# GNN edge phase with dense edge tiles at fixed addresses, and a segment sum over (tile, block) visits with a ring of message tiles

## The chip, the cores and the metric

The kernel runs on one core of a Trainium2 chip. The metric is the device time of one execution in microseconds (us). The kernel before took 1274.54 us (median of three runs, 1274.37 to 1276.86).

## The reference

Layer norm of x (1250 nodes x 512), one message-passing layer over 20,000 edges sorted by their destination node, then a small mixture-of-experts part. All is in float32. The part that matters here is the message layer:

```python
edge_feat = jnp.concatenate([x[src], x[dst], edge_attr], axis=-1)
h = mish(edge_feat @ W1 + b1)
messages = mish(h @ W2 + b2)
agg = jax.ops.segment_sum(messages, dst, num_segments=x.shape[0])
u = mish(jnp.concatenate([x, agg], axis=-1) @ W3 + b3)
```

## The kernel before

Four phases follow one another with a barrier of all engines between them: `prologue`, `edge_phase`, `node_phase` and `ffn_phase`. The change touches the first two.

**Tiles.** The nodes lie in 10 blocks of 125. The edges are worked on in tiles of 128. Before, each tile holds edges of one block only, so every block begins a new tile and its last tile may be partly empty: 20,000 edges need at most `TILES` = 166 tiles, that is 83 pairs (`PAIRS`), and the loops always run over all 83. The DVE works out in the prologue where each tile starts (`tiles_reached`, `tile_blocks`, `tile_starts`, L488 to L509): `start_i`, `block_i` and `block_off`.

**Prologue.** It normalises x and makes two tables in DRAM, `src_table` = x @ W1[src part] and `dst_table` = x @ W1[dst part] + b1 (PE L581 to L600, ten row tiles; ACT L404 and DVE L558 evict, SP L260 and L263 store). GpSimd copies the edge attributes and the indices to DRAM scratch (L336, L337), with a tail of padding (L299, L300).

**Edge phase.** It is one pipeline of steps s, written out in full for every engine, from `FIRST` = -5 to `LAST` = `PAIRS` + 4 = 87. Each step works at several pairs at different stages. For the pair p:
- SP at s = p - 5 reads the two tile starts into registers (L684) and issues for each tile one load of indices (L685) and two of edge attributes (L687).
- GpSimd gathers rows of `src_table` at s = p - 2 (L702) and adds rows of `dst_table` at s = p - 1 (L709). The gather buffer has three slots and a slot is free when PE has transposed it (`gath_read`).
- PE transposes the attributes at s = p - 1 (L897), transposes the gathered rows into the PSUM banks of linear 1 at s = p (`gathered_bank`, L836) and adds the attribute product (L870, L871). The second half of the banks waits for `summed`, since segment sums of an earlier pair are in that bank.
- ACT and DVE compute mish for linear 1 (DVE L813, L786, L806, L818) and for linear 2 (DVE L821, L809, L826).
- PE does linear 2 with split high and low parts at s = p + 1 (`hi_tile` of the second tile) and s = p + 2 (`hi_tile` of the first, both `lo_tile`; L841, L844).
- DVE rounds the message (`msg_hi`, L826), and DVE (L801) and GpSimd (L717) make the low parts `msg_lo`, two buffers of two tiles each.
- The segment sum is at s = p + 4: DVE makes a one-hot matrix from the local destination numbers (`dloc`, L790, and L795), PE multiplies it with the two parts of the message (L882, L883), and DVE adds the result to the block's rows of `agg`: `add_sums(m, 0)` in the same step, `add_sums(o, 1)` of the pair before early in the next step. Each `add_sums` first reads the block number from SBUF into a register (L769), then waits for the sum, then adds (L774).

At the end of the phase W3 is loaded (L690) and split into high and low parts: ACT L764, DVE L829, GpSimd L720, spread over the last steps by `act_parts`, `dve_parts` and `pool_parts`.

**Order of the work around the change.** PE in one step: `hi_tile(g, 0)`, first half of the gathered banks, second half (after `summed`), `lo_tile(g, 0)`, the eight attribute matmuls, `lo_tile(g, 1)`, the four sum matmuls, `hi_tile(r, 1)`, two attribute transposes. DVE in one step: L781, `add_sums(o, 1)`, L786, L790, L795, L801, L806, L809, L813, `add_sums(m, 0)`, L818, L821, L826. GpSimd in one step: two L702, two L709, one L717.

## Time and profile before

| | us |
|---|---|
| median of three runs | 1274.54 |
| lowest, highest | 1274.37, 1276.86 |
| the profiled execution, its time | 1276.67 |
| its span in the trace | 1275.1 |
| PE busy | 1120.8 (88%) |
| DVE busy | 990.7 (78%) |
| ACT busy | 874.9 (69%) |
| GpSimd busy | 739.4 (58%) |

All times are of one profiled execution, in us unless marked ns. PE is the TensorE matmul stream, PEld its weight loads (they overlap matmuls), DVE the VectorE, ACT the ScalarE, POOL the GpSimd, SPq, DVEq and PEldq the instruction queues of their engines. In the rows, L and a number is a line of the kernel. "[0.59 <-issue]" behind a row says how long the engine had stood idle before it and what ended that; "issue" means that nothing which the trace shows was waited for. Matmuls are pipelined: each row of a 512-column matmul shows about 0.39 us, but one starts 0.23 us after the other. The edge phase runs from 97.7 to 924 us of the span.

### The profile page before, as it was taken

To read this page: it belongs to the slowest core of one execution; us is meant where nothing else is said; L and a number is where in the kernel's file an instruction comes from. 1 tells how busy PE (TensorE), PEld (TensorE's weight loads), DVE (VectorE), ACT (ScalarE), POOL (GpSimd) and SP (SyncE) were. 2 spreads that over 40 slices of the span, in tenths; PEclk is the share of its full clock that TensorE was granted. 3 is DMA by queue.
4 is the path that set the end of the run, shared out by engine and by line. 5 is a ranking of instruction groups with operands and counts; after the bars stand their busy time and mean duration, and the time that the engine had idled before them with its cause. 6 is when DMAs were issued, how large, how long until landed. Compare 5 with 4: busy or idle time off the path is not lost. (4 is left out here: it accounts for less than half of the span.)

```text
span 1275.1 us, 21174 instructions
## 1 busy us (share of the span) xinstructions
PE 1120.8 (88%) x5823; PEld 911.8 (72%) x5824; DVE 990.7 (78%) x1793; ACT 874.9 (69%) x1061; POOL 739.4 (58%) x589
## 2 busy tenths in 40 slices
PE   3991999999999999999999999999579995679974
PEld 2761788888878888888888888888357774568863
DVE  6640699999999999999999999999848875643356
ACT  2211798999989999999899998999544541433332
POOL 3235677777777777777777777773221210644420
PEclk9995999999999999999999999999779995669975
DMA  5725666666666666666666666664020112734435
GB/s 164 271 89 124 141 128 125 130 124 129 128 126 129 125 128 127 126 131 124 128 127 128 130 127 125 129 123 116 0 67 25 49 38 68 212 88 132 132 121 182
DMA packets 138654, 153.51 MB, mean 120 GB/s; under 512 B 80635, under 2 KB 89226, under 8 KB 138477
## 3 DMA queue, kind: packets, MB, share of 16 engines
q0 software_dynamic: 40912, 101.69, 37.9%
q1 hardware_dynamic: 97629, 50.66, 15.5%
q8 instruction: 42, 0.69, 0.2%
q14 instruction: 55, 0.45, 0.1%
q10 hardware_dynamic: 16, 0.02, 0.0%
HBM read 141.74 MB, written 15.66 MB: 123 GB/s over the span
## 5 line engine op out<-in xcount | busy, mean ns | idle before, releaser
L702 POOL DMA_INDIRECT gath<-src_table,idx_sl x166 | 223.6, 1347 | 143.0 <-PE ps L836 84.9
L709 POOL DMA_INDIRECT gath<-dst_table,idx_sl x166 | 274.8, 1655 | 50.4 <-issue 50.4
L841 PE MATMUL ps<-W2h,hTh 128*128 128x512 f32 x664 | 262.6, 395 | 0.0
L841 PE MATMUL ps<-W2l,hTh 128*128 128x512 f32 x664 | 262.2, 395 | 0.0
L841 PE MATMUL ps<-W2h,hTl 128*128 128x512 f32 x664 | 188.5, 405 | 0.0
L717 POOL TENSOR_TENSOR msg_lo<-act,msg_hi 128x512 fp32r<-128x512 f32 x83 | 152.5, 1837 | 33.2 <-DVE msg_hi L826 33.2
L774 DVE TENSOR_TENSOR agg<-agg,ps 125x512 f32 x166 | 114.0, 687 | 57.8 <-issue 42.9
L841 PEld LDWEIGHTS ps<-W2l,hTh 128*128 128x128 f32 x664 | 124.7, 188 | 29.2
L841 PEld LDWEIGHTS ps<-W2h,hTh 128*128 128x128 f32 x664 | 125.1, 188 | 26.3
L733 ACT ACTIVATE act<-ps 128x1024 f32<-128x1024 f32 x83 | 85.2, 1027 | 72.0 <-issue 47.0
L836 PE MATMUL ps<-ident,gath 128*128 128x128 f32 x664 | 103.6, 282 | 29.2 <-DMA gath<-dst_table,idx_sl 14.6
L841 PEld LDWEIGHTS ps<-W2h,hTl 128*128 128x128 f32 x664 | 113.0, 189 | 15.5
L836 PEld LDWEIGHTS ps<-ident,gath 128*128 128x128 f32 x664 | 77.3, 142 | 58.7 <-DVE agg L774 26.3
L786 DVE SCALAR_TENSOR_TENSOR act<-act,ps 128x1024 f32<-128x1024 f32 x83 | 100.8, 1214 | 2.1 <-ACT act L752 2.1
L809 DVE SCALAR_TENSOR_TENSOR act<-act,ps 128x1024 f32<-128x1024 f32 x83 | 100.6, 1212 | 2.1 <-ACT act L761 2.0
L818 DVE TENSOR_TENSOR hTl<-act,hTh 128x1024 fp32r<-128x1024 f32 x83 | 101.0, 1217 | 0.0
L744 ACT ACTIVATE act<-act,half_col 128x1024 f32<-128x1024 f32 x83 | 95.8, 1154 | 2.7
L758 ACT ACTIVATE act<-act,half_col 128x1024 f32<-128x1024 f32 x83 | 95.6, 1152 | 2.7
L742 ACT ACTIVATE act<-act 128x1024 f32<-128x1024 f32 x83 | 88.1, 1062 | 3.8 <-issue 2.8
L761 ACT ACTIVATE act<-act 128x1024 f32<-128x1024 f32 x83 | 88.1, 1062 | 2.6
L755 ACT ACTIVATE act<-act 128x1024 f32<-128x1024 f32 x83 | 87.0, 1049 | 3.5 <-DVE act L821 3.5
L752 ACT ACTIVATE act<-act 128x1024 f32<-128x1024 f32 x83 | 87.4, 1053 | 0.0
(315 smaller groups left out, 2589.3 us busy)
## 6 DMA issues: line engine op xcount, KB each, us to landing
f_w_raw<-in_L_ffn_w_dram SPq DMA_DIRECT2D x32, 512.0 KB, 4.7
ea_sl<-ea_scr SPq DMA_DIRECT2D x332, 32.0 KB
ea_scr<-in_edge_attr_dram POOLq DMA_DIRECT2D x1, 5000.0 KB
w_raw<-in_L_gnn_W_dram SPq DMA_DIRECT2D x3, 1024.0 KB, 13.2
idx_sl<-idx_scr SPq DMA_DIRECT2D x166, 1.5 KB
gath<-src_table,idx_sl POOLq DMA_INDIRECT x166
gath<-dst_table,idx_sl POOLq DMA_INDIRECT x166
x_raw<-in_x_dram SPq DMA_DIRECT2D x5, 448.0 KB
```

Of the source, the lines that this page charges most:

```text
L702: pool.indirect_dma_start(out=gath[:, k, j, :], out_offset=None, in_=src_table[:, :], in_offset=bass.IndirectOffsetOnAxis(ap=idx_sl[:, p % ...
L709: pool.indirect_dma_start(out=gath[:, k, j, :], out_offset=None, in_=dst_table[:, :], in_offset=bass.IndirectOffsetOnAxis(ap=idx_sl[:, p % ...
L717: nc.gpsimd.tensor_tensor(msg_lo[:, p % 2, 1], act2[:, p % A2, 1], f32(msg_hi[:, p % 2, 1]), ALU.subtract).then_inc(S["msg_lo1_ready"], 1)
L742: nc.scalar.activation(a1, a1, ACT.Square).then_inc(S["sq1"], 1)
L744: nc.scalar.activation(a1, a1, ACT.Ln, bias=half_col[:], scale=0.5).then_inc(S["ln1"], 1)
L758: nc.scalar.activation(a2, a2, ACT.Ln, bias=half_col[:], scale=0.5).then_inc(S["ln2"], 1)
L774: nc.vector.tensor_tensor(row, row, sums(p)[0:NB, j, :], ALU.add).then_inc(S["summed"], 1)
L786: nc.vector.scalar_tensor_tensor(out=h, in0=h, scalar=1.0, in1=ps_1[:, r % 2], op0=ALU.subtract, op1=ALU.mult).then_inc(S["h_ready"], 1)
L809: nc.vector.scalar_tensor_tensor(out=a3, in0=a3, scalar=1.0, in1=ps_2[:, f % 2], op0=ALU.subtract, op1=ALU.mult).then_inc(S["msg_ready"], 1)
L818: nc.vector.tensor_tensor(hTl[:, r % 2], h, f32(hTh[:, r % 2]), ALU.subtract).then_inc(S["h_lo"], 1)
L836: ins = nc.tensor.matmul(ps_1[:, p % 2, d, j * P:(j + 1) * P], lhsT=gath[:, p % GA, j, d * P:(d + 1) * P], rhs=ident[:], is_transpose=True ...
L841: return nc.tensor.matmul(ps_2[:, p % 2, j, :], part[:, p % 2, d, j * P:(j + 1) * P], weights[:, d, :], start=False, stop=last)
```

## The change

- The edges are laid out densely: tile t is edges 128t to 128t + 127, without regard to blocks. `TILES` is now 158, so `PAIRS` is 79. The addresses of a tile's loads are known when the program is built; SP reads no register and issues one load of indices and two of attributes for a pair instead of two and four.
- A tile may hold edges of more than one block. The segment sum therefore runs over `VISITS` = 166 (tile, block) pairs, 83 pairs of visits (`SUMS`). All stages but the sum run over 79 pairs, the sums over 83, and `LAST` stays 87.
- A message tile can be needed by later visits, so `msg_hi` and `msg_lo` are rings of 14 tiles. The ring slot of each visit (`slot_i`) is read by PE into a register, two reads a step, ahead of the gathered banks; the sum matmuls address their moving operand with it.
- The local destination numbers `dloc` of all visits are made once, in the prologue: a DRAM copy of the destinations by tile (`dst_scr`), two indirect gathers of its rows by visit on GpSimd, two DVE copies, two PE transposes and one DVE subtraction. The DVE instruction L790 of every step goes away, and with it SP's wait on it.
- To make room for the rings, `eaT`, `ea_sl` and `act1` lie over the W3 high part and `hTh`, `hTl` over the W3 low part. The splitting of W3 waits for their last use, and its parts are ordered anew over the last steps.

```diff
@@ constants @@
-TILES = (EDGES + BLOCKS * (P - 1)) // P
+TILES = 2 * ((EDGES + 2 * P - 1) // (2 * P))
+ROWS = TILES * P
+VISITS = TILES + BLOCKS - 2
+VISITS += VISITS % 2
+RING = 14
@@ gnn_ffn_kernel @@
-        ea_scr = dram("ea_scr", (EDGES + P, EDIM), F32)
-        idx_scr = dram("idx_scr", (EDGES + P, 3), I32)
+        ea_scr = dram("ea_scr", (ROWS, EDIM), F32)
+        idx_scr = dram("idx_scr", (ROWS, 2), I32)
+        dst_scr = dram("dst_scr", (TILES, P), I32)
...
-        start_i = sb("start_i", [P, TILES], I32, edge_ctx)
-        block_i = sb("block_i", [P, TILES], I32, edge_ctx)
-        block_off = sb("block_off", [P, TILES], F32, edge_ctx)
+        slot_i = sb("slot_i", [P, VISITS], I32, edge_ctx)
+        block_i = sb("block_i", [P, VISITS], I32, edge_ctx)
+        dloc = sb("dloc", [P, VISITS], F32, edge_ctx)
@@ prologue: gpsimd @@
-                c.inc(nc.gpsimd.tensor_copy(rec_i[:, :, 2], dst_i[:]))
...
+                    pool.dma_start(dst_flat[0:EDGES].rearrange("(p j) -> p j", p=EP), dst_i[:]).then_inc(S["dst_out"], 16)
...
-            pool.wait_ge(S["tail_out"], 32)
+                pool.wait_ge(S["dst_out"], 16)
+            pool.wait_ge(S["tail_out"], 48)
...
+            pool.wait_ge(S["col_ready"], 1)
+            for n, rows in enumerate(VISIT_PARTS):
+                pool.indirect_dma_start(out=vdst_i[0:rows, n, :], out_offset=None, in_=dst_scr[:, :],
+                                        in_offset=bass.IndirectOffsetOnAxis(ap=tile_col[0:rows, n:n + 1], axis=0)).then_inc(S["vdst_in"], 16)
@@ prologue: vector @@
-            def tile_starts():
...
+            def visit_tiles():
+                c.step(nc.vector.tensor_reduce(out=behind[:], in_=reached[:].rearrange("p b v -> p v b"), axis=AX_X, op=ALU.add))
+                c.inc(nc.vector.tensor_tensor(tile_f[:], iota_v[:], behind[:], ALU.subtract))
+                c.inc(nc.vector.tensor_tensor(slot_f[:], iota_s[:, 0:VISITS], behind[:], ALU.subtract))
                 c.inc(nc.vector.tensor_copy(block_i[:], block_f[:]))
                 c.inc(nc.vector.tensor_scalar(block_off[:], block_f[:], float(NB), None, ALU.mult))
                 c.wait()
+                nc.vector.tensor_scalar(tile_f[:], tile_f[:], float(TILES - 1), None, ALU.min).then_inc(S["tiles_set"], 1)
+                c.step(nc.vector.tensor_scalar(wrap_f[:], slot_f[:], 0.0, float(RING), ALU.is_lt, ALU.mult))
+                c.step(nc.vector.tensor_tensor(slot_i[:], slot_f[:], wrap_f[:], ALU.add))
+            def visit_columns():
+                dve.wait_ge(S["col_ps"], 1)
+                for n, rows in enumerate(VISIT_PARTS):
+                    ins = nc.vector.tensor_copy(tile_col[0:rows, n:n + 1], ps_m[0:rows, 128 + n:129 + n])
+                ins.then_inc(S["col_ready"], 1)
+            def visit_nodes():
+                dve.wait_ge(S["vdst_in"], 32)
+                for n, rows in enumerate(VISIT_PARTS):
+                    ins = nc.vector.tensor_copy(vdst_f[0:rows, n, :], vdst_i[0:rows, n, :])
+                ins.then_inc(S["vdst_ready"], 1)
+                dve.wait_ge(S["vdst_ps"], 1)
+                c.step(nc.vector.tensor_tensor(dloc[:], ps_m[:, 256:256 + VISITS], block_off[:], ALU.subtract))
@@ prologue: tensor @@
-            steps(pe, step, 0, BLOCKS, 4, BLOCKS - 1)
+            steps(pe, step, 0, BLOCKS - 1, 4, BLOCKS - 3)
+            pe.wait_ge(S["tiles_set"], 1)
+            for n, rows in enumerate(VISIT_PARTS):
+                ins = nc.tensor.transpose(ps_m[0:rows, 128 + n:129 + n], tile_f[0:1, n * P:n * P + rows], ident[0:1, 0:1])
+            ins.then_inc(S["col_ps"], 1)
+            step(0, BLOCKS)
+            pe.wait_ge(S["vdst_ready"], 1)
+            for n, rows in enumerate(VISIT_PARTS):
+                ins = nc.tensor.transpose(ps_m[:, 256 + n * P:256 + n * P + rows], vdst_f[0:rows, n, :], ident[0:rows, 0:rows])
+            ins.then_inc(S["vdst_ps"], 1)
@@ edge_phase @@
+        def over_w3h(name, shape, part):
+            return nc.alloc_sbuf_tensor_at(name, shape, F32, offset=T["w3h_at"] + part * HID * 4)
+        idx_sl = sb("idx_sl", [P, IN, 2, 2], I32)
+        eaT = w3h[:, 0, :].rearrange("p (s e) -> p s e", s=2)
+        ea_sl = over_w3h("ea_sl", [P, IN, 2, 2 * EDIM], 1)
         gath = sb("gath", [P, GA, 2, HID])
-        act1 = sb("act1", [P, 2, KC, E2])
         act2 = sb("act2", [P, A2, 2, HID])
-        hTh = sb("hTh", [P, 2, KC, E2], F32R)
-        hTl = sb("hTl", [P, 2, KC, E2], F32R)
-        msg_hi = sb("msg_hi", [P, 2, 2, HID], F32R)
-        msg_lo = sb("msg_lo", [P, 2, 2, HID], F32R)
-        dloc = sb("dloc", [P, TILES])
+        msg_hi = sb("msg_hi", [P, RING, HID], F32R)
+        msg_lo = sb("msg_lo", [P, RING, HID], F32R)
...
+        hTh, hTl = half_of(w3l, 0), half_of(w3l, KC)
+        act1 = over_w3h("act1", [P, 2, KC, E2], KC)
...
-        FIRST, LAST = -5, PAIRS + 4
+        SUMS = VISITS // 2
+        FIRST, LAST = -5, SUMS + 4
...
+        def visited(m):
+            return 0 <= m < SUMS
+        def ring(p):
+            return slice(2 * p % RING, 2 * p % RING + 2)
+        def ring_free(p):
+            return p - 1 if 2 * p >= RING else 0
...
-        act_parts = {PAIRS: (7, 0, 1, 2), PAIRS + 1: (3, 4, 5, 6)}
-        dve_parts = {PAIRS + 1: (0, 1), PAIRS + 2: (2,), PAIRS + 3: (3, 4, 5, 6)}
-        pool_parts = {PAIRS + 1: (7,)}
+        act_parts = {PAIRS: (0, 1, 2, 3), PAIRS + 1: (4, 5, 6, 7)}
+        dve_parts = {PAIRS + 2: (0, 1), PAIRS + 3: (2, 3), PAIRS + 4: (4, 5)}
+        pool_parts = {PAIRS + 3: (7, 6)}
@@ edge_phase: sync, gpsimd @@
-                        sp.wait_ge(S["dst_ready"], p - IN + 1)
-                    for j in range(2):
-                        first = sp.value_load(start_i[0:1, p * 2 + j:p * 2 + j + 1], min_val=0, max_val=EDGES)
-                        sp.dma_start(idx_sl[:, k, j, :], idx_scr[bass.ds(first, P), :]).then_inc(idx_in[k], 16)
-                        for half in range(2):
-                            sp.dma_start(ea_sl[:, k, j, half * EDIM:(half + 1) * EDIM], ea_scr[bass.ds(first, P), :]).then_inc(ea_in[k], 16)
+                    edges = slice(p * E2, (p + 1) * E2)
+                    sp.dma_start(idx_sl[:, k], idx_scr[edges, :].rearrange("(j p) r -> p j r", p=P)).then_inc(idx_in[k], 16)
+                    for half in range(2):
+                        sp.dma_start(ea_sl[:, k, :, half * EDIM:(half + 1) * EDIM], ea_scr[edges, :].rearrange("(j p) d -> p j d", p=P)).then_inc(ea_in[k], 16)
...
-                    pool.wait_ge(*loaded(idx_in, IN, p, 32))
+                    pool.wait_ge(*loaded(idx_in, IN, p, 16))
...
-                    if p >= 2:
-                        pool.wait_ge(S["sum_ps"], p - 1)
-                    nc.gpsimd.tensor_tensor(msg_lo[:, p % 2, 1], act2[:, p % A2, 1], f32(msg_hi[:, p % 2, 1]), ALU.subtract).then_inc(S["msg_lo1_ready"], 1)
+                    need(pool, S["sum_ps"], ring_free(p))
+                    nc.gpsimd.tensor_tensor(msg_lo[:, ring(p)][:, 1], act2[:, p % A2, 1], f32(msg_hi[:, ring(p)][:, 1]), ALU.subtract).then_inc(S["msg_lo1_ready"], 1)
                 for w in pool_parts.get(s, ()):
+                    pool.wait_ge(S["lin2_ps"], PAIRS)
@@ edge_phase: vector @@
-                if exists(l):
-                    dve.wait_ge(*loaded(idx_in, IN, l, 32))
-                    nc.vector.tensor_tensor(dloc[:, 2 * l:2 * l + 2], idx_sl[:, l % IN, :, 2], block_off[:, 2 * l:2 * l + 2], ALU.subtract).then_inc(S["dst_ready"], 1)
-                if exists(m):
-                    dve.wait_ge(S["dst_ready"], m + 1)
+                if visited(m):
...
                     dve.wait_ge(S["msg_hi_ready"], m + 1)
-                    if m >= 2:
-                        dve.wait_ge(S["sum_ps"], m - 1)
-                    nc.vector.tensor_tensor(msg_lo[:, m % 2, 0], a4[:, 0], f32(msg_hi[:, m % 2, 0]), ALU.subtract).then_inc(S["msg_lo0_ready"], 1)
+                    need(dve, S["sum_ps"], ring_free(m))
...
-                if exists(m):
+                if visited(m):
...
-                    if f >= 2:
-                        dve.wait_ge(S["sum_ps"], f - 1)
+                    need(dve, S["sum_ps"], ring_free(f))
                     dve.wait_ge(S["msg_ready"], f + 1)
-                    nc.vector.tensor_copy(msg_hi[:, f % 2], a3).then_inc(S["msg_hi_ready"], 1)
+                    nc.vector.tensor_copy(msg_hi[:, ring(f)], a3).then_inc(S["msg_hi_ready"], 1)
                 for w in dve_parts.get(s, ()):
+                    dve.wait_ge(S["lin2_ps"], PAIRS)
@@ edge_phase: tensor @@
                 if exists(g):
                     hi_tile(g, 0)
+                if visited(m):
+                    slots = [pe.value_load(slot_i[0:1, 2 * m + j:2 * m + j + 1], min_val=0, max_val=RING - 1) for j in range(2)]
...
                     lo_tile(g, 1).then_inc(S["lin2_ps"], 1)
-                if exists(m):
+                if visited(m):
                     pe.wait_ge(S["onehot_ready"], m + 1)
-                    pe.wait_ge(S["msg_lo0_ready"], m + 1)
-                    pe.wait_ge(S["msg_lo1_ready"], m + 1)
+                    pe.wait_ge(S["msg_lo0_ready"], min(m + 1, PAIRS))
+                    pe.wait_ge(S["msg_lo1_ready"], min(m + 1, PAIRS))
                     pe.wait_ge(S["h_ready"], min(m + 4, PAIRS))
                     o = sums(m)
                     for j in range(2):
-                        nc.tensor.matmul(o[0:NE, j, :], onehot[:, m % 2, j, :], msg_hi[:, m % 2, j, :], start=True, stop=False)
-                        ins = nc.tensor.matmul(o[0:NE, j, :], onehot[:, m % 2, j, :], msg_lo[:, m % 2, j, :], start=False, stop=True)
+                        for lo, part in enumerate((msg_hi, msg_lo)):
+                            ins = nc.tensor.matmul(o[0:NE, j, :], onehot[:, m % 2, j, :], part[:, bass.ds(slots[j], 1), :].rearrange("p a n -> p (a n)"),
+                                                   start=lo == 0, stop=lo == 1)
                     ins.then_inc(S["sum_ps"], 1)
```

## Rows read from the trace of the kernel before

**Rows 1.** Busy time by stretch: window, length, PE, PEld, DVE, ACT, POOL, PE clock, DMA share, GB/s

```profile
200.00:872.20 672.20, 662.05 (x3442) 540.97 (x3441) 619.20 (x931) 614.69 (x646) 529.22 (x359) 1.00 0.65 127
...
915.00:920.00 5.00, 1.90 (x4) 1.17 (x4) 3.00 (x5) 0.00 (x0) 1.64 (x1) 0.50 0.00 0
```

**Rows 2.** Timeline of DVE: start, length, engine, line, operation; the first sum's addition of three steps

```profile
159.36 0.69 DVE L774 TENSOR_TENSOR agg<-agg,ps 125x512 f32 x1 [0.23 <-PE ps L883]
...
872.23 0.69 DVE L774 TENSOR_TENSOR agg<-agg,ps 125x512 f32 x1
...
881.26 0.69 DVE L774 TENSOR_TENSOR agg<-agg,ps 125x512 f32 x1 [0.23 <-PE ps L883]
```

**Rows 3.** Timeline of all engines over one step of the edge phase

```profile
506.24 0.69 DVE L774 TENSOR_TENSOR agg<-agg,ps 125x512 f32 x1
...
508.40 1.68 POOL L709 DMA_INDIRECT gath<-dst_table,idx_sl  x1 [0.30 <-issue]
...
509.30 0.43 DVE L781 TENSOR_TENSOR eaT<-ps,eaT 64x256 fp32r<-64x256 f32 x1
...
510.31 0.69 DVE L774 TENSOR_TENSOR agg<-agg,ps 125x512 f32 x1 [0.59 <-issue]
510.34 1.37 PE L836 MATMUL ps<-ident,gath 128*128 128x128 f32 x8
...
511.06 0.42 PEld L836 LDWEIGHTS ps<-ident,gath 128*128 128x128 f32 x4 [0.35 <-DVE agg L774]
```

**Rows 4.** Line L769, DVE's register reads in two stretches: ns min/median/max, first and last start

```profile
L769 DVEq TENSOR_LOAD <-block_i x1: 943/943/943, 508.9 to 508.9; - x1
...
L769 DVEq TENSOR_LOAD <-block_i x1: 300/300/300, 874.9 to 874.9; - x1
```

**Rows 5.** PE's register reads of the last phase (L1691), all and one, and the matmuls around

```profile
L1691 PEldq FUSED_REGOPS  x56: 42/151/168, 1130.4 to 1221.0; - x56
L1691 PEldq TENSOR_LOAD <-expert_i x35: 297/303/493, 1129.8 to 1220.7; - x35
...
L1691 PEldq TENSOR_LOAD <-expert_i x1: 310/310/310, 1151.8 to 1151.8; - x1
...
1152.20 0.28 PE L1718 MATMUL f_ps_n<-w1Th,xgTl 128*128 x1
1152.72 0.52 PE L1698 MATMUL f_ps_t<-ident,xg 128*128 128x128 f32 x3 [0.24 <-issue]
```

**Rows 6.** Timeline of the start of the edge phase

```profile
98.72 0.40 SPq L685 DMA_DIRECT2D idx_sl<-idx_scr  x1
...
101.53 0.34 SPq L685 DMA_DIRECT2D idx_sl<-idx_scr  x1
...
103.43 1.06 POOL L702 DMA_INDIRECT gath<-src_table,idx_sl  x1 [24.62 <-DMA idx_sl<-idx_scr]
...
111.47 1.61 POOL L709 DMA_INDIRECT gath<-dst_table,idx_sl  x1 [0.31 <-issue]
...
119.57 1.97 PE L836 MATMUL ps<-ident,gath 128*128 128x128 f32 x8 [14.61 <-DMA gath<-dst_table,idx_sl]
```

**Rows 7.** Timeline of DVE over the last steps of the edge phase

```profile
907.93 2.36 DVE L829 TENSOR_TENSOR w1l_w3l<-w_raw,w1h_w3h 128x512 fp32r<-128x512 f32 x2
...
917.32 0.68 DVE L801 TENSOR_TENSOR msg_lo<-act,msg_hi 128x512 fp32r<-128x512 f32 x1
920.29 0.69 DVE L774 TENSOR_TENSOR agg<-agg,ps 125x512 f32 x1 [2.29 <-PE ps L883]
920.90 2.49 DVE L829 TENSOR_TENSOR w1l_w3l<-w_raw,w1h_w3h 128x512 fp32r<-128x512 f32 x4
923.31 0.68 DVE L774 TENSOR_TENSOR agg<-agg,ps 125x512 f32 x1
```

**Rows 8.** Timeline of the end of the prologue

```profile
93.50 0.69 DVE L558 COPY tabs<-ps_b 125x512 f32<-125x512 f32 x1 [5.49 <-PE ps_b L600]
94.22 0.76 SPq L263 DMA_DIRECT2D dst_table<-tabs  x2
```

More of the change, by code:

```diff
@@ L481, in first_edges @@
[L481 removed]
+                c.step(nc.vector.tensor_copy(tfirst[:], cnt_i[:]))
+                c.step(nc.vector.scalar_tensor_tensor(out=shared[:], in0=tfirst[:], scalar=float(P), in1=first[:, 0:BLOCKS],
+                                                      op0=ALU.mult, op1=ALU.is_lt))
+                c.step(nc.vector.tensor_tensor_scan(out=extra[:], data0=ones[:, 0:BLOCKS], data1=shared[:], initial=0.0,
@@ L482, in first_edges @@
                                                     op0=ALU.mult, op1=ALU.add))
-                c.step(nc.vector.scalar_tensor_tensor(out=off[:], in0=tbase[:], scalar=-float(P), in1=first[:, 0:BLOCKS + 1],
-                                                      op0=ALU.mult, op1=ALU.add))
-                c.inc(nc.vector.tensor_tensor(doff[:], off[:, 1:BLOCKS + 1], off[:, 0:BLOCKS], ALU.subtract))
-            def tiles_reached():
-                for b in range(BLOCKS):
-                    c.inc(nc.vector.tensor_scalar(reached[:, b, :], iota_t[:], tbase[:, b + 1:b + 2], None, ALU.is_ge))
+                c.step(nc.vector.tensor_tensor(vbase[:], tfirst[:], extra[:], ALU.add))
```

105 lines of the change are left out of this document (62 added, 43 removed).

## The prediction

> **What bounds the kernel now.** I read the busy times by stretch first. Between 200 and 872.2 us PE is busy for 662 of 672 us at a granted clock of 1.00, DVE for 619 [rows 1]. So the edge loop is the place, and two engines are near full in it. The timeline of DVE gives its period: `add_sums(m, 0)` of step 4 starts at 159.36 and that of step 80 at 872.23 [rows 2], 76 steps apart, so a step takes 712.87 / 76 = 9.38 us. One step in the timeline shows what closes the loop [rows 3]. PE has its last sum matmul done, DVE adds the first sum at 506.24, works through L818, L821, L826 and L781 and adds the second sum only at 510.31. PE has begun the first half of the gathered banks at 510.34 and holds the second half until 511.06, released by that addition. From there it runs without a gap to the next sum. So the period is one PE half plus one DVE half. DVE stood 0.59 us idle before the second addition with nothing to wait for: its register read took 943 ns, from 508.9 on, where the same read takes 300 ns at 874.9 [rows 4], and the step from 872.23 to 881.26 is 9.03 us [rows 2]. Each pair of tiles costs one step, whatever it holds.
>
> **Part 1: four pairs fewer.** Loads, gathers, both linears and both mish run over 79 pairs instead of 83; the sums keep 83. `LAST` stays 87, so four steps of the full kind become steps with a sum alone. Four full steps go: 4 x 9.38 = 37.5 us [rows 2]. What replaces them is part 3.
>
> **Part 2: what is added to and taken from each remaining step.** L790 leaves DVE. It lay between the second addition and the first, where DVE has a wait on PE (0.23 us at two of the rows) [rows 2], so it is off the loop and I count 0. SP's register reads and half its DMAs go; SP's loads run pairs ahead: 0. The ring only moves waits on `sum_ps` that were long met: 0.
>
> PE gets two register reads a step, between `hi_tile(g, 0)` and the gathered banks. No row shows PE reading a register in this phase. The last phase does: the read takes 303 ns, the register operations after it 151 [rows 5], so a pair of reads is 2 x 0.45 = 0.91 us. They are in PE's instruction queue and not in the array. The question is whether that queue is far enough ahead. It is held by the wait on `summed` in front of the attribute transposes, met when the first addition ends, 506.24 + 0.69 = 506.93 [rows 3]. Then it issues 22 instructions (two transposes and nine matmuls with their weight loads). Four weight loads with their four transposes took 0.42 us, 0.052 each [rows 3], so it reaches the reads at 506.93 + 1.15 = 508.1 and is through at 509.0. The banks need it near 510.1, and before that it waits anyway for L781, which ends at 509.73 [rows 3]. Cover: 1.1 us. If both reads were as slow as DVE's worst (943 ns), they would end at 508.1 + 2 x (0.94 + 0.15) = 510.3; the first half of the banks would start 0.2 us late and the second half, held until 511.06, would not move. In the last phase a read began at 1151.8 while matmuls before it still started at 1152.20, so a read doesn't wait for the array; but the 0.24 us gap ahead of 1152.72 shows what it costs where the queue is only 0.4 us ahead [rows 5]. I take 0, with 0 to 0.1 us a step as the bounds of the forecast. A price far above is a rival below.
>
> The Trainium skill (TensorE: Matmul & The Clock Gate, the table at its head) gives TensorE a queue of 64 instructions; the 22 fit, and by it the sum stays as it is.
>
> **Part 3: the drain.** Steps 79 to 82 of the new kernel are like 83 to 86 of the old. The two L829 of step 84 (2.36 us [rows 7]) leave the path to step 86; one more comes in at step 85 (0.6), and I take 2.2 us as gained there, since the sum of step 85 waited for PE behind them: the addition at 920.29 would be at 918.1 in the old count. Then come four steps with a sum alone. In each, DVE's second addition of the pair before starts about 0.75 after the first (it waits for its end, 0.69), the one-hot matrix starts 0.60 after that and takes 0.41 (the distances of one step of DVE), and from the end of DVE's last input to the addition after the sum passed 920.29 - (917.32 + 0.68) = 2.29 us, with PE at half clock [rows 7, 1]. Sum: 0.75 + 0.60 + 0.41 + 2.29 = 4.05. PE's register reads are under that. In two of the steps two L829 lie in the chain too; alone four took 2.49, and beside GpSimd two took 2.36 [rows 7], so 1.2 to 2.4, taken as 1.8. The last first-addition is at 918.1 + 4 x 4.05 + 2 x 1.8 = 937.9, the phase ends at 937.9 + 0.75 + 0.68 = 939.3, where it ended at 923.31 + 0.68 = 924.0 [rows 7]. The drain costs 15.3 us. If PE held full clock, its four matmuls would start 0.23 apart instead of twice that and a step would be 0.9 shorter, with fast L829s 10.5 us in all; with slow ones and half a microsecond of exposed reads a step 18.5 us.
>
> **Part 4: the fill.** Before, GpSimd's first gather waits for the second index load, issued at 101.53, 2.8 us after the first at 98.72, and the register read ahead of the first took about 1 us. GpSimd starts 1.9 after that issue (103.43) [rows 6]. With one index load for a pair and no read, the gather starts at about 97.7 + 1.9 = 99.6, 3.8 us sooner. The second pair's indices no longer hold it back either, so the queue would reach L709 at 104.9, not 111.47. That one waits for its source gathers, about 4.6 us behind the end of their issue (as from the end of the second L709, 114.94, to PE at 119.57 [rows 6]): 102.0 + 4.6 = 106.6. All behind moves by 111.5 - 106.6 = 4.9 us. Bounds: 2.8 (the one issue alone) to 6.6.
>
> **Part 5: the prologue.** DVE has about 1 us of new small work in the tile tables and two copies, and had 5.49 us idle before its last eviction at 93.50 [rows 8]. So the two indirect gathers go out near 89, in 2.6 us of issue, and land near 94 to 95, by the 4.6 us above. Two DVE copies, two transposes and a subtraction follow, some 1.5 us: 96 to 96.5. The barrier is held by SP's last table store, issued at 94.22 and over near 97.5, since the first index load stands at 98.72 behind a read [rows 8, 6]. Covered; PE's two tiny transposes ahead of its last row tile shift that store by 0.3 to 0.5. I take +0.5; if the gathers land 3 us later the chain ends the phase: up to +3.5.
>
> **Sum.** -37.5 + 0 + 15.3 - 4.9 + 0.5 = -26.6 us. The profiled execution took 1276.67, so 1250.1 for it; it is 2.1 us above the median of the runs, and against 1274.54 I predict 1247.9. With the bounds (drain 10.5 to 18.5, fill -6.6 to -2.8, prologue 0 to 3.5, PE reads 0 to 0.1 x 79 = 8) the forecast's own range is 1241 to 1264.
>
> **Rivals.**
> *PE's register reads stand in the way (slower).* If a read is served only when the matmuls ahead are done, the two start at the end of `hi_tile`, 510.34, and the banks at 511.25. The first half takes 0.25, the second starts at 511.5 instead of about 511.1: 0.45 us a step, 79 x 0.45 = 36 us, total 1248 + 36 = 1284. It turns the sign from 0.34 us a step on. For it: the gap at 1152.72. Against: the read at 1151.8 ran beside matmuls [rows 5]. Chance 0.12.
> The Trainium skill (DMA: Bandwidth & Descriptors, Latency and other measured facts) puts the floor of a tensor load at about 600 ns, twice the 303 ns in this trace. By it two reads take 1.5 us; the sum stays, since 508.1 + 1.5 is still ahead of 510.1, and this rival would cost 0.6 us a step more.
> *PE's reads lengthen DVE's (about the same).* They run at 508.1 to 509.0, DVE's at 508.9, and that one is on the loop. Half of its 0.64 us stretch again would be 0.32 x 79 = 25 us: 1273. No row speaks for it but the fact that DVE's read varies at all [rows 4]. Chance 0.05.
> *DVE's slow read goes away (faster still).* It is slow where GpSimd's second L709 runs (508.40 to 510.08 [rows 3]) and fast at 874.9, when no gather is issued. If the new timing parts the two, a step takes 9.03: 75 x 0.35 = 26 us, 1222. But GpSimd is paced by PE's banks in the same loop as before, so they should meet again. Chance 0.08.
> *It doesn't do what it says.* The counts 79 and 83 are constants of the program, so the steps must go; only the price of the rest can be wrong. No chance of its own.
>
> **How the numbers follow.** Forecast 0.75, rivals 0.12, 0.05 and 0.08. The range 1224 to 1269 holds the forecast, its slips beyond its own range, and part of the second and the third rival; left out are the slower rival and most of the fastest. About 0.2% (2.5 us) is what a measurement can tell from no change. Faster by more: 0.75 + 0.08 + 0.02 = 0.85; within: 0.03; slower: 0.12.
>
> **What the profile would show.** The first addition of step 4 to that of step 76 in 72 x 9.38 = 675 us; PE's second bank half still released by DVE's second addition, and the queue's reads over before L781 ends; sum-only steps 4 to 6 us apart at the end; L702 first at about 2 us behind the barrier; the barrier released by SP's store. The prediction falls if the step is over 9.7 us, or if the last steps take over 6 us each.

## The result, and the profile after

The changed kernel takes 1254.32 us (median of 4 runs, 1252.38 to 1255.62) where the kernel before takes 1274.5: a ratio of 0.9836, with a 95% interval of 0.9818 to 0.9854. The forecast was 1247.9, faster, with a range of 1224 to 1269. The profiled execution took 1255.11 us, its span is 1253.5 (before: 1275.1).

The edge phase first. Busy time by stretch in the changed kernel (window, length, PE, PEld, DVE, ACT, POOL, PE clock, DMA share, GB/s), to be laid beside [rows 1]:

```profile
200.00:833.70 633.70, 615.31 (x3211) 505.25 (x3211) 574.15 (x803) 571.63 (x603) 492.96 (x335) 1.00 0.63 125
890.00:902.00 12.00, 6.20 (x12) 3.47 (x12) 4.59 (x9) 0.00 (x0) 0.00 (x0) 0.50 0.00 0
```

PE is busy for 97.1% of the full steps, where it was for 98.5%, and DVE for 90.6% against 92.1%: both are a little emptier. The clock is 1.00 as before, so each step has become longer by idle time of the engines. The timeline of DVE (start, length, engine, line, operation) says by how much; these are the first sum's additions of steps 4, 76 and 77, as in [rows 2]:

```profile
151.41 0.69 DVE L845 TENSOR_TENSOR agg<-agg,ps 125x512 f32 x1 [0.20 <-PE ps L951]
...
833.79 0.69 DVE L845 TENSOR_TENSOR agg<-agg,ps 125x512 f32 x1 [0.20 <-PE ps L951]
842.76 0.69 DVE L845 TENSOR_TENSOR agg<-agg,ps 125x512 f32 x1 [0.21 <-PE ps L951]
```

(833.79 - 151.41) / 72 = 9.477 us a step, against 9.38. One such step in the timeline of all engines, for [rows 3]:

```profile
483.25 0.69 DVE L845 TENSOR_TENSOR agg<-agg,ps 125x512 f32 x1 [0.19 <-PE ps L951]
...
485.35 1.75 POOL L778 DMA_INDIRECT gath<-dst_table,idx_sl  x1 [0.30 <-issue]
485.48 0.36 SPq L754 DMA_DIRECT2D idx_sl<-idx_scr  x1
485.88 1.87 SPq L756 DMA_DIRECT2D ea_sl<-ea_scr  x2
486.31 0.43 DVE L852 TENSOR_TENSOR w1h_w3h<-ps,w1h_w3h 64x256 fp32r<-64x256 f32 x1
487.32 0.60 PE L902 MATMUL ps<-ident,gath 128*128 128x128 f32 x4
487.40 0.69 DVE L845 TENSOR_TENSOR agg<-agg,ps 125x512 f32 x1 [0.66 <-issue]
488.14 0.66 PE L902 MATMUL ps<-ident,gath 128*128 128x128 f32 x4 [0.22 <-DVE agg L845]
```

The loop is closed as it was (its period is one half of PE's step plus one half of DVE's): the second half of PE's gathered banks is released by DVE's second addition. That one comes 4.15 us after the first (4.07 before), with 0.66 us of idle time ahead of it in place of 0.59. And SP now issues the loads of a later pair at 485.48 and 485.88, alongside DVE's block read. Here are the register reads, DVE's in this step and at 850.9 to 852.0 (for [rows 4]), then both of PE's, which are new (name, count: ns min/median/max, first and last start):

```profile
L840 DVEq TENSOR_LOAD <-block_i x1: 1030/1030/1030, 485.9 to 485.9; - x1
...
L840 DVEq TENSOR_LOAD <-block_i x2: 303/306/309, 850.9 to 852.0; - x2
...
L925 PEldq TENSOR_LOAD <-slot_i x2: 297/304/310, 484.1 to 484.9; - x2
L925 PEldq FUSED_REGOPS  x2: 151/151/151, 484.5 to 485.3; - x2
```

PE's reads cost what [rows 5] said and are over at 485.5, before DVE's begins. DVE's has grown from 943 ns to 1030.

The start of the phase, for [rows 6, 8]:

```profile
93.14 0.76 SPq L283 DMA_DIRECT2D dst_table<-tabs  x2
...
96.75 0.39 SPq L754 DMA_DIRECT2D idx_sl<-idx_scr  x1
...
98.81 0.98 POOL L771 DMA_INDIRECT gath<-src_table,idx_sl  x1 [9.14 <-DMA idx_sl<-idx_scr]
...
104.51 1.60 POOL L778 DMA_INDIRECT gath<-dst_table,idx_sl  x1 [0.94 <-DMA gath<-src_table,idx_sl]
...
111.83 1.97 PE L902 MATMUL ps<-ident,gath 128*128 128x128 f32 x8 [11.31 <-DMA gath<-dst_table,idx_sl]
```

PE has its first gathered rows 7.74 us earlier than before, and the first addition of step 4 comes 159.36 - 151.41 = 7.95 us earlier. About one microsecond of that is the prologue's, whose last store is issued at 93.14, not 94.22. The start isn't the same in every execution: in eight traces of the changed kernel and its variants with all gathers and additions in place, step 4's first addition lies between 150.21 and 152.03. At the end stand the steps with a sum alone, in a form that the kernel before did not have:

```profile
893.53 0.69 DVE L845 TENSOR_TENSOR agg<-agg,ps 125x512 f32 x1 [2.36 <-PE ps L951]
894.43 0.69 DVE L845 TENSOR_TENSOR agg<-agg,ps 125x512 f32 x1 [0.21 <-DVE agg L845]
895.04 0.41 DVE L862 TENSOR_TENSOR onehot<-iota_n,dloc 128x252 fp32r<-128x252 f32 x1
895.60 0.79 PE L951 MATMUL ps<-msg_hi,onehot 128*126 x1 [2.21 <-DVE onehot L862]
...
897.81 0.69 DVE L845 TENSOR_TENSOR agg<-agg,ps 125x512 f32 x1 [2.36 <-PE ps L951]
```

The last two take 4.28 us each. PE idles 2.21 us of one until the one-hot matrix is there, and DVE idles 2.36 until PE has its four matmuls done at half clock. The phase ends at 902.99 + 0.69 = 903.68.

The account of the spans, in us:

| stretch | before | after | difference | forecast |
| --- | --- | --- | --- | --- |
| start to step 4's first addition | 159.36 | 151.41 | -7.95 | -4.9 + 0.5 |
| step 4 to step 80 (before), 76 (after) | 712.87 | 682.38 | -30.49 | -37.5 |
| from there to the end of the phase | 51.76 | 69.89 | +18.13 | +15.3 |
| the rest of the kernel | 351.11 | 349.82 | -1.29 | 0 |
| sum | 1275.1 | 1253.5 | -21.6 | -26.6 |

The 7 us missing in the second line are 0.098 us in each of 72 steps. That is what most of the experiments are about. The last line of the table explains 5.0 of the 6.4 us between forecast and median; most of the other 1.4 comes from the profiled execution before, which lay 2.1 us above its median, where the one after lay 0.8 above. All ratios below are to the kernel before, measured beside each run (medians of 1272.9 to 1274.5 us), and all "steps" are (first addition of step 76 - that of step 4) / 72 unless said otherwise.

### The profile page after: what moved, and what is told of

It reads as the page before. It is cut to its first block and busy times, and to the rows that moved or that the text cites. A ratio compares the mean times of both kernels' runs of the same rounds, so it can differ in the third digit from the quotient of the medians.

```text
span 1253.5 us, 19768 instructions
## 1 busy us (share of the span) xinstructions
PE 1084.6 (87%) x5651; PEld 884.2 (71%) x5652; DVE 958.0 (76%) x1678; ACT 837.7 (67%) x1025; POOL 713.5 (57%) x574
## 3 DMA queue, kind: packets, MB, share of 16 engines
q0 software_dynamic: 39280, 97.61, 36.2%
## 5 line engine op out<-in xcount | busy, mean ns | idle before, releaser
L907 PE MATMUL ps<-W2h,w1l_w3l 128*128 128x512 f32 x1264 | 426.6, 398 | 0.0
L778 POOL DMA_INDIRECT gath<-dst_table,idx_sl x158 | 265.2, 1679 | 48.6 <-issue 47.1
L771 POOL DMA_INDIRECT gath<-src_table,idx_sl x158 | 207.9, 1316 | 126.1 <-PE ps L902 86.0
L907 PEld LDWEIGHTS ps<-W2h,w1l_w3l 128*128 128x128 f32 x1264 | 227.3, 189 | 38.6
L907 PE MATMUL ps<-W2l,w1l_w3l 128*128 128x512 f32 x632 | 248.2, 393 | 0.0
L907 PEld LDWEIGHTS ps<-W2l,w1l_w3l 128*128 128x128 f32 x632 | 119.0, 188 | 27.2
L802 ACT ACTIVATE act<-ps 128x1024 f32<-128x1024 f32 x79 | 81.2, 1027 | 74.8 <-PE ps L939 74.8
L884 DVE TENSOR_TENSOR w1l_w3l<-act,w1l_w3l 128x1024 fp32r<-128x1024 f32 x79 | 96.2, 1218 | 0.0
L951 PE MATMUL ps<-msg_hi,onehot 128*126 x166 | 69.0, 416 | 22.9 <-DVE msg_lo L867 12.2
L830 ACT ACTIVATE act<-act 128x1024 f32<-128x1024 f32 x79 | 83.9, 1062 | 2.5
L811 ACT ACTIVATE act<-act 128x1024 f32<-128x1024 f32 x79 | 83.1, 1052 | 3.7 <-DVE act L879 3.6
L824 ACT ACTIVATE act<-act 128x1024 f32<-128x1024 f32 x79 | 83.0, 1051 | 3.5 <-DVE act L887 3.5
L821 ACT ACTIVATE act<-act 128x1024 f32<-128x1024 f32 x79 | 83.3, 1055 | 0.0
L808 ACT ACTIVATE act<-ps 128x1024 f32<-128x1024 f32 x79 | 81.2, 1028 | 0.0
```

The lines of the kernel that those rows point to most:

```text
L771: pool.indirect_dma_start(out=gath[:, k, j, :], out_offset=None, in_=src_table[:, :], in_offset=bass.IndirectOffsetOnAxis(ap=idx_sl[:, p % ...
L778: pool.indirect_dma_start(out=gath[:, k, j, :], out_offset=None, in_=dst_table[:, :], in_offset=bass.IndirectOffsetOnAxis(ap=idx_sl[:, p % ...
L830: nc.scalar.activation(a2, a2, ACT.Exp, scale=-1.0).then_inc(S["quot2"], 1)
L884: nc.vector.tensor_tensor(hTl[:, r % 2], h, f32(hTh[:, r % 2]), ALU.subtract).then_inc(S["h_lo"], 1)
L907: return nc.tensor.matmul(ps_2[:, p % 2, j, :], part[:, p % 2, d, j * P:(j + 1) * P], weights[:, d, :], start=False, stop=last)
```

## Experiments: what lengthens the step

**PE's register reads removed.**

```diff
-slots = [pe.value_load(slot_i[0:1, 2 * m + j:...], ...) for j in range(2)]
+slots = [(2 * min(m, PAIRS - 1) + j) % RING for j in range(2)]
```

> The changed kernel, with one thing taken out: TensorE reads no ring positions; its two reads of a step are replaced by constants (so the sums of tiles that lie in two blocks take the wrong message tile; the amount of work is the same). Full steps of the changed kernel are 9.48 us apart where 9.38 was predicted. Theory A (SyncE's DMA issues now lie on VectorE's second block read, and the reads of TensorE cost nothing): the step stays at 9.45 to 9.50 us and the execution at about 1255. Rival B (TensorE's two reads, 0.3 us each, lengthen VectorE's read or the path): the step goes back to 9.38, 72 x 0.10 = 7 us off, about 1248. If the reads were in the sum-only steps' chain too, those would be shorter than 4.28 us.

Measured: 1253.93 us, ratio 0.9849 (0.9832 to 0.9865), step 9.464. The sum-only steps went from 4.28 to 4.20. The reads take 0.01 us of a step and 0.08 of a sum-only one, so rival B fell.

**SP's issues held back, first try and second.** In both, SP gets one wait more ahead of its loads of pair p:

```diff
 sp.wait_ge(S["eaT_ps"], p - IN + 1)
+if p >= 10:                                        # second try: p >= 9
+    sp.wait_ge(S["summed"], 2 * (p - 10) + 2)      # second try: p - 9
```

> The changed kernel, with one wait more: SyncE issues the loads of a later pair only after VectorE's second addition of the step (in the changed kernel it issues them beside VectorE's second block read, which takes 1.03 to 1.10 us there against 0.94 to 0.97 before). Theory A (SyncE's issues lengthen that read): the read goes back to 0.94 to 0.97 us, the step to 9.38, the time by 7 us to about 1248. Rival B (it isn't SyncE): the read stays at 1.03 to 1.10 and the step at 9.48; about 1255. If the loads came too late for their pair, steps would show waits on them; they run pairs ahead, so I expect none.

Measured: 1253.99 us, ratio 0.9844 (0.9827 to 0.986), step 9.473. The wait asked for an addition of the step before and was always met, so SP's issues stayed where they were. The trial says nothing on its theory. The second one does:

> The changed kernel, with one wait more, a pair later than in the trial before, in which SyncE's issues had not moved (they still began 0.01 us after VectorE's second block read): SyncE now issues the loads of a later pair behind VectorE's second addition. Theory A (SyncE's issue, when it begins with the read, adds 0.1 us to it): the read goes from 1.07 back to 0.95 us, as in the three steps at 286.5, 817.7 and 827.0 of the changed kernel that took 0.93 to 0.96 (two of them without an issue of SyncE near); the step goes from 9.47 to 9.38, about 7 us off, 1247. Rival B: the read stays at 1.03 to 1.08 and the step at 9.47; 1254.

Measured: 1246.99 us, ratio 0.9798 (0.9777 to 0.9819). The additions of steps 4 and 76 stand at 151.76 and 826.03, a step of 9.365. The timeline shows SP behind the second addition; below it, DVE's reads between 200 and 800 us have a largest value of 967 ns, where the changed kernel has 1098:

```profile
483.45 0.69 DVE L847 TENSOR_TENSOR agg<-agg,ps 125x512 f32 x1 [0.57 <-issue]
...
484.23 0.36 SPq L756 DMA_DIRECT2D idx_sl<-idx_scr  x1
```

```profile
L842 DVEq TENSOR_LOAD <-block_i x128: 300/322/967, 201.0 to 797.1; - x128
```

and in the changed kernel:

```profile
L840 DVEq TENSOR_LOAD <-block_i x127: 299/317/1098, 201.4 to 798.7; - x127
```

Theory A stands: SP's issue beside the read was the 7 us. The slow reads are again at 0.95 us in the median, where the changed kernel has 1.07 and the kernel before 0.94, and (9.477 - 9.365) x 72 = 8.1 us are gone from the steps. By the times alone the gain is less sure: 7.3 us between the medians, 4.8 by the two ratios (0.9836 and 0.9798), whose intervals just meet. Before the change, SP stood there in register reads (L684, 508.5 to 509.1 in the step of [rows 3]) and issued its index load at 509.65, 0.7 us into DVE's read; the change removed those, and in nearly every step its issues moved to 0.4 us before the read's start and to the start itself.

**One gather of destination rows in a pair instead of two.** The range in L778 is cut to j = 0, and the waits on `both_gath` count 16 instead of 32.

> The changed kernel, with the second tile of each pair left without its gather of destination rows (its result is wrong for those edges; all other work is the same). It is the gather whose issue on GpSimd (1.7 us) lies on VectorE's second block read. Theory A (that issue is what makes the read slow, 0.3 us without it): the read falls to about 0.3 to 0.4 us and the step to 9.0 to 9.1, the time to about 1255 - 72 x 0.4 = 1226. Rival B (the read is slow for another reason, the table in memory or the operation before it): read about 1.0, step 9.48, about 1255. Rival C: the gather left is now issued later and lies on the read in its place: a read between 0.6 and 1.0.

Measured: 1253.39 us, ratio 0.9839 (0.9822 to 0.9855), step 9.468. My theory A fell: the read is as slow without GpSimd's issue beside it. Nor did C come true: the gather left was issued at 784.1 for 1.58 us, and the read began at 786.5. The lines of the gather and of the read say so, and the DMA share in two windows (columns as in the first fence) shows what did meet the read:

```profile
L778 POOL DMA_INDIRECT gath<-dst_table,idx_sl x1: 1576/1576/1576, 784.1 to 784.1; - x1
...
L840 DVEq TENSOR_LOAD <-block_i x1: 1084/1084/1084, 786.5 to 786.5; - x1
```

```profile
786.00:786.40 0.40, 0.40 (x4) 0.30 (x3) 0.40 (x2) 0.33 (x3) 0.00 (x0) 1.00 0.00 0
786.50:787.50 1.00, 1.00 (x6) 0.81 (x5) 0.86 (x2) 1.00 (x2) 0.49 (x1) 1.00 0.94 164
```

The DMA engines are idle until 786.4, and at 0.94 during the read: the rows of the gather begin to move 2.3 us after the start of its issue, just there.

**No gather of destination rows.**

```diff
-for j in range(2):
-    pool.indirect_dma_start(out=gath[:, k, j, :], in_=dst_table[:, :], ..., compute_op=ALU.add)...
```

> The changed kernel, with both gathers of destination rows left out (the rows gathered are those of the sources alone, so the result is wrong; TensorE, VectorE and ScalarE do the same work). In the trial with one gather left per pair, no issue of GpSimd lay near VectorE's second read (the last had ended 0.8 us before it), and yet it took 1.07 us. What was there each time is the data of the destination rows (packets of 2048 bytes, added to what is in memory), which begins to flow 0.1 us before the read. Theory A (the start of that flow holds the read): without it the second read takes 0.3 us, though SyncE still issues with it, and the step falls to 8.97 to 9.05, the time to about 1220. Rival B (SyncE's issue, or the data of the source rows, holds it): the read stays near 1 us and the step at 9.4 or more. Rival C: GpSimd, free earlier, issues the source rows' gathers onto the read, and the read is slow by these: between 0.3 and 1.

Measured: 1211.11 us, ratio 0.9514 (0.9495 to 0.9533), step 8.988. All reads are fast, though SP issues its index load at 406.17 and its attributes at 406.57, beside a read at 406.6:

```profile
L832 DVEq TENSOR_LOAD <-block_i x134: 299/304/317, 199.9 to 798.5; - x134
```

So SP's issue alone holds nothing. It adds 0.1 us to a read that is already held.

**Destination rows not added.** `compute_op=ALU.add` is taken out of L778.

> The changed kernel, in which the gathers of destination rows no longer add to the rows in memory but take their place (the sources' share of each edge is lost, so the result is wrong); number, order, addresses and size of all gathers are the same. The first block read of a step begins as the data of the source rows begins to flow (packets of 4096 bytes) and takes 0.31 us; the second begins as that of the destination rows does (2048 bytes, added) and takes 1.07. Theory A (the addition in memory is what holds the read): plain destination rows hold it no more than source rows do; the second read takes 0.3 us, the step is 8.97 to 9.05, the time about 1220. Rival B (any flow that starts beside that read holds it, or GpSimd's issue or SyncE's does, and the first read is only lucky in its place): the read stays at 0.9 to 1.1 and the step at 9.38 to 9.48; about 1254.

Measured: 1218.7 us, ratio 0.9576 (0.956 to 0.9592), step 8.994.

```profile
L839 DVEq TENSOR_LOAD <-block_i x133: 299/307/326, 203.5 to 797.0; - x133
```

```profile
485.20:485.50 0.30, 0.30 (x3) 0.25 (x2) 0.30 (x2) 0.30 (x3) 0.30 (x1) 1.00 0.75 287
485.50:485.90 0.40, 0.40 (x4) 0.31 (x3) 0.40 (x1) 0.40 (x2) 0.09 (x1) 1.00 0.19 72
```

The sizes are as A expected, but the trial doesn't separate as cleanly as I meant: plain gathers are issued faster (1.02 us for the first, 1.57 before), so their rows had been moving for some time when the read came at 485.57. So no run puts a plain flow onto the second read itself. Other reads of the traces help. In the changed kernel, the first read of the next step does begin with a flow, that of source rows, which are not added, and takes 311 ns; the first reads of the other steps between 200 and 800 us take 0.30 to 0.32 as well. And in the kernel before there are reads that come when added rows have been moving for a while: that at 162.0, 0.7 us behind the first of them, takes 309 ns, and that at 621.8, 0.44 us behind the first, 556 ns.

The changed kernel, windows and read:

```profile
491.00:491.50 0.50, 0.50 (x4) 0.41 (x3) 0.50 (x1) 0.50 (x1) 0.20 (x2) 1.00 0.04 9
491.80:492.10 0.30, 0.30 (x3) 0.25 (x2) 0.30 (x2) 0.30 (x1) 0.30 (x1) 1.00 0.89 164
```

```profile
L840 DVEq TENSOR_LOAD <-block_i x1: 311/311/311, 491.8 to 491.8; - x1
```

The kernel before, windows and read:

```profile
161.00:161.30 0.30, 0.30 (x5) 0.21 (x3) 0.30 (x2) 0.30 (x1) 0.30 (x1) 1.00 0.15 20
161.70:162.00 0.30, 0.30 (x3) 0.25 (x2) 0.30 (x2) 0.30 (x2) 0.30 (x1) 1.00 0.83 143
```

```profile
L769 DVEq TENSOR_LOAD <-block_i x1: 309/309/309, 162.0 to 162.0; - x1
```

```profile
621.00:621.35 0.35, 0.35 (x5) 0.31 (x4) 0.35 (x1) 0.35 (x1) 0.35 (x1) 1.00 0.00 0
621.40:622.40 1.00, 1.00 (x6) 0.81 (x5) 0.97 (x3) 1.00 (x3) 1.00 (x1) 1.00 0.94 104
```

```profile
L769 DVEq TENSOR_LOAD <-block_i x1: 556/556/556, 621.8 to 621.8; - x1
```

Taken together: a block read that begins within 0.1 us of the first row of an added flow takes 0.88 to 1.1 us, and one that begins 0.45 us into it 0.56 to 0.71. One that begins 0.7 us into it takes 0.31 or 0.39 us, and one that meets no such beginning 0.3. All that are held end at about the same place: 1.0 to 1.05 us behind the flow's first row in the kernel before and in the trial above with SP's issues behind the addition, and 1.1 to 1.2 with SP's issues beside them. So it looks less like a read made longer by a fixed amount than like one held until the flow is about 1 us old. How the two are tied inside the chip no run here shows.

## Experiments: what a step and a read are worth

**DVE's block reads removed.** `b` becomes `(p * 2 + j) // 17`.

> The changed kernel, with VectorE's block reads taken out: the addition of a sum goes to block tile // 17, a constant (so some tiles are added to the wrong block; the work is the same). TensorE's reads stay. Theory A (the loop is one half of TensorE's step plus one half of VectorE's, and the latter contains the slow second read, about 1.05 us with what is behind it, at a VectorE that stands idle 0.7 us): the step falls to 9.38 - 0.35 = 9.0 us or a little under, as in the steps without gathers (8.97 to 9.03), and the time by 72 x 0.45 = 32 us or a little more, to about 1220. Rival: TensorE's own work (9.2 of 9.38 us busy) is the bound as soon as the read is gone, and the step falls only to 9.2 to 9.3: about 1240.

Measured: 1218.51 us, ratio 0.9569 (0.9553 to 0.9585), step 8.989. The slow read closes the loop, and behind it PE's own work is the bound at 8.99, below the 9.2 of the rival: PE has no gap left (columns as in the first fence).

```profile
200.00:790.00 590.00, 589.58 (x3154) 497.86 (x3153) 578.27 (x789) 561.53 (x592) 458.72 (x329) 1.00 0.66 132
```

**The kernel before with 158 tiles.** `TILES = 158`.

> The kernel before, with 158 tiles instead of 166 and nothing else changed (the edges of the last 8 tiles are left out). It measures the change's first part by itself, four full steps fewer: by the prediction's sum 4 x 9.38 = 37.5 us less, about 1237. With it the other terms of the change are the difference to 1254: the drain (+18), the step's +0.1 x 72, the fill (-8). If it comes out at 1250 or more, a step isn't the price of a pair and the sum is wrong at its base.

Measured: 1238.66 us where the kernel before took 1272.9 beside it, ratio 0.9729 (0.9711 to 0.9748): 34.2 us for four pairs. Its step is (837.85 - 159.46) / 72 = 9.422, 0.04 longer than the 9.38 before: its slow reads take 0.98 us in the median (up to 1.02), where they took 0.94. 4 x 9.38 = 37.5, less 72 x 0.042 = 3.0, is 34.5. Nothing in that program moved but the number of tiles; why its reads are 0.04 longer is open. The last 51.7 us are as before.

**The kernel before, with both reads of a pair early.**

```diff
+if exists(m):
+    read_blocks(m)          # both value_load of block_i, kept for add_sums
 if exists(p):
     dve.wait_ge(S["exp1"], p + 1)
```

> The kernel before, with both block reads of a pair moved: VectorE takes them together ahead of the first addition, in front of its wait for the first activation, and keeps the second value for the second addition. Nothing stands then between the attribute rows' low part and the second addition. Theory A (VectorE's slow second read closes the loop): the step falls from 9.38 to about 9.0, 76 x 0.37 = 28 us off, about 1246. Rival B: the early reads fall on another flow of gathered rows and are slow there too, and VectorE, with little slack, is late for the next wait of TensorE: a gain of 0 to 10 us. Rival C: TensorE is the bound at once: step 9.2, 1260.

Measured: 1246.72 us, ratio 0.9797 (0.9776 to 0.9818), step 9.026; between 200 and 800 us DVE's reads take 316 ns at most. This alone gives a little more than the change did (ratio 0.9797 against 0.9836, with intervals that meet at 0.9818). One early read, in one of the last steps with gathers, is slow:

```profile
L772 DVEq TENSOR_LOAD <-block_i x1: 650/650/650, 841.4 to 841.4; - x1
```

GpSimd had begun to issue a gather of destination rows at 839.40, and its first rows begin at 841.64, inside this read. So the new place is no protection by itself; it is good because the flows begin elsewhere.

**The changed kernel, with both reads early.** The same edit, under `visited(m)`.

> The changed kernel, with both block reads of a pair moved ahead of the first addition, in front of VectorE's wait for the first activation, as was done with the kernel before (there the step went from 9.38 to 9.03 us, the time from 1272.9 to 1246.7). Theory A (the data of the destination rows begins to flow at the place where the second read stood; at the new place no such flow begins): all reads take 0.3 us, SyncE's issues touch none of them, and the step is 8.99 to 9.03, as without any block read (8.99). That is 72 x 0.46 = 33 us under the changed kernel's 1254: 1219 to 1223. Rival B (the early reads of the changed kernel, whose GpSimd queue has another order of loads, meet the flow anyway): step above 9.2, over 1235.

Measured: 1222.37 us, ratio 0.9594 (0.9581 to 0.9608). The additions of steps 4 and 76 are at 151.58 and 800.48, a step of 9.012. Theory A again; the longest of the 166 reads takes 0.34 us.

**The changed kernel, one-hot matrices early in the drain.**

```diff
-if visited(m):
-    if m >= 2: dve.wait_ge(S["sum_ps"], m - 1)
-    ... onehot[:, m % 2] ...
+for v in ((m,) if m < PAIRS else ()) + ((m + 1,) if m + 1 >= PAIRS else ()):
+    if visited(v):
+        if v >= 2: dve.wait_ge(S["sum_ps"], v - 1)
+        ... onehot[:, v % 2] ...
```

> The changed kernel, with the one-hot matrix of the next pair made ahead of the first addition of this one in the steps that hold a sum alone (two buffers are there). In them the chain of the changed kernel is: second addition, one-hot matrix, four matmuls at half clock, first addition, 4.28 us a step, with TensorE idle for 2.2 us of each. Theory A (that chain sets the end of the phase): TensorE has its next matrix when it ends a sum, and a step takes about 2.1 to 2.6 us; four of them save 6 to 8 us, less what the two steps with the last weight parts keep (5.18 each, in which VectorE has 1.3 us more): about 1248. Rival B (TensorE's register reads or the weight parts bound these steps): no step under 3.5, a gain of under 3 us.

Measured: 1246.95 us, ratio 0.9788 (0.9774 to 0.9801); from step 76 to the end of the phase it is 61.05 us instead of 69.89. PE goes from sum to sum:

```profile
889.41 0.68 DVE L845 TENSOR_TENSOR agg<-agg,ps 125x512 f32 x1
889.64 0.79 PE L952 MATMUL ps<-msg_hi,onehot 128*126 x1 [0.67 <-DVE onehot L863]
...
891.65 0.79 PE L952 MATMUL ps<-msg_hi,onehot 128*126 x1
891.85 0.69 DVE L845 TENSOR_TENSOR agg<-agg,ps 125x512 f32 x1 [0.53 <-PE ps L952]
...
893.67 0.69 DVE L845 TENSOR_TENSOR agg<-agg,ps 125x512 f32 x1 [0.23 <-PE ps L952]
```

The last two steps take 2.44 and 1.82 us, those with weight parts 2.74 where I had them keep 5.18.

**Both edits in the changed kernel.**

> Both edits of the two kernels beside it in one: the block reads early, and the one-hot matrices early in the steps with a sum alone. They lie in different parts of the phase (the full steps, and the last steps), so their gains should add: about 33 + 6 = 39 us under the changed kernel, 1213 to 1217. Rival: the two share VectorE's wait in the last steps (the early reads stand ahead of the additions there too) and a part of the second gain is lost: 1218 to 1221.

Measured: 1214.12 us (1212.21 to 1215.07), ratio 0.9526 (0.9513 to 0.9539). It is 40.2 us under the changed kernel; the two edits alone gave 32.0 and 7.4 (by the ratios, which take out how the kernel before varied from run to run, 39.5, 30.8 and 6.1). So the gains add. It leaves nothing out, and is the fastest of all versions here that don't: 4.7% under the kernel before and 3.2% under the changed one.

## Why the prediction was right in sign and 6 us low

The result lies inside the forecast's own range of 1241 to 1264. By its steps:

- **Part 1, right in mechanism, 3 us too large in size.** Forecast -37.5, measured alone -34.2. The steps went as reckoned; the step that remained was not quite 9.38.
- **Part 2, PE's reads at 0: right.** The queue's cover was even larger than the 1.1 us of the sum: the reads of the step at 483.25 end at 485.5, and the banks' first weight load starts at 487.09. Taking the reads out moved the step by 0.01. (The 943 ns taken as DVE's worst read was not the worst: the kernel before has reads of up to 970.) The two rivals that hung on them, 1284 and 1273, have no part in the result. The first would have been 0.45 a step.
- **Part 2, SP at 0: this step failed.** I wrote that half of SP's DMAs go and that its "loads run pairs ahead: 0". That asked only whether a load comes too late, and not what its issue would lie beside once SP's reads ahead of it were gone. It came to lie on the one read of DVE that closes the loop. Measured: 0.1 us a step, 7 us, which SP's wait gave back (a step of 9.365, so what else the change does to a step, L790 and the ring among it, comes to about nothing, as forecast; 1246.99, under a microsecond from the forecast, though the errors of other terms offset each other in it: the start came out 3 us lower and the drain 2.8 higher than forecast).
- **The slow read named, its cause not.** The rival "DVE's slow read goes away" put it down to GpSimd's second gather issue, since it runs beside it in [rows 3]. It doesn't hang on that issue: with the issue away from it the read stayed slow, with the rows gone it was fast. Its size was right. I had 26 us and 0.35 a step for a fast read; the early reads gave 0.35 in the kernel before and 0.465 in the changed one.
- **Part 3, within its range, but 2.8 us short, and not where it was thought.** Sum-only steps were put at 4.05 and took 4.28: the second addition starts 0.90 after the first, not 0.75 (its read and wait add 0.21 idle), and PE's part took 2.36 from the end of the one-hot, not 2.29. They held half clock, as taken. The two with weight parts were put at 5.85 and took 5.18, so the four together were 0.9 us under the forecast. What was too small lies ahead of them: from step 76 to 82 the forecast had 918.1 - 872.23 = 45.9 us, and it took 883.17 - 833.79 = 49.4. I had counted 2.2 us as gained there by moving weight parts. The stretch up to 874.12 did gain 1.4 (7.31 us where 8.68 stood, 905.43 to 914.11), but the next one, up to 883.17, took 9.05 where its counterpart before (914.11 to 920.29) took 6.18. Two weight parts of DVE (L895, 2.35 us) stand in it ahead of the second addition, where one stood before (0.68), and the low part of the message (L867) takes 1.75 us beside GpSimd's weight parts (L789, 877.09 to 880.20), where it took 0.68. The total of 18.1 lies within 10.5 to 18.5.

```profile
874.12 0.69 DVE L845 TENSOR_TENSOR agg<-agg,ps 125x512 f32 x1 [0.64 <-PE ps L951]
...
875.33 2.35 DVE L895 TENSOR_TENSOR w1l_w3l<-w_raw,w1h_w3h 128x512 fp32r<-128x512 f32 x2
...
879.01 1.75 DVE L867 TENSOR_TENSOR msg_lo<-act,msg_hi 128x512 fp32r<-128x512 f32 x1
883.17 0.69 DVE L845 TENSOR_TENSOR agg<-agg,ps 125x512 f32 x1 [2.42 <-PE ps L951]
```

- **Part 4 and 5, too small.** Forecast -4.4, measured -7.95, outside -6.6. GpSimd's first gather came at 98.81 (forecast 99.6) and the first of destination rows at 104.51 (106.6): the source rows landed about 3.5 us behind the end of their issue and not 4.6. The prologue's chain was covered, as forecast, but its last store came 1.1 us earlier where I had it 0.5 later; no run shows why, and the start varies by 1.8 us between traces as it is.
- **The Trainium skill.** PE's two reads at its floor for a tensor load (DMA: Bandwidth & Descriptors, Latency and other measured facts) would have taken 1.2 us for the loads alone, by an estimate from that figure. The trace shows 297 and 310 ns, half of it. By the floor the reads end 0.6 us later and are still covered, so this case would not have told the difference in time.

## What to carry to other kernels

When a change takes instructions off a queue that is off the critical path, ask where the ones behind them move to, and what lies on the path there. Here removing SP's register reads, and with them the delay of its DMA issues, cost 0.1 us in each of 72 steps. A register read on an engine that closes a loop is best taken well ahead, where nothing waits for it: that was worth 32 us, more than the change itself. And a step that holds one stage alone still runs the whole chain of that stage; where two buffers are there, make its input a step early.

## What the chip showed that I had not expected

- A register read by DVE takes 300 ns, and 880 to 1100 where it begins together with rows that a gather adds in memory. GpSimd's issue of the gather need not lie beside it; its rows do, some 2.2 us behind the start of the issue. Reads that begin later into the flow are held less (556 ns at 0.44 us, 309 at 0.7), so that these end about 1.0 us behind its first row.
- SP's DMA issue that begins with such a held read adds 0.1 us (1.07 against 0.95 in the median). One that begins 0.4 to 0.8 us into it adds nothing (0.94 in the kernel before), nor does one beside a read that isn't held (304 ns in the median of 134).
- Gathers that add take longer to issue and to move: 1.57 and 1.75 us of GpSimd for the issues of a pair against 1.02 and 1.50 without the addition, and 36.2% against 26.6% of the DMA engines' time for the same 97.61 MB of GpSimd's queue over the whole kernel (spans of 1253.5 and 1216.8 us).
